# A decoder of two layers on one core: the order of work at four stage fronts

## The reference, cut to what matters

```
layer 0: causal self attention, 16 heads of 16, rotary factor on q and k
         GEGLU with the context as weights
         mixture: 1 shared + 8 routed experts (width 512), top 2, silu(x w1) * (x w3) @ w2
layer 1: full self attention, 16 heads of 16
         cross attention to the context (softmax over the queries)
         mixture: 8 experts (width 1024), top 2 with a masked softmax ("phi" routing)
```

## Time and profile before

| | |
|---|---|
| median of 3 runs | 1590.3 us (1586.99 to 1592.11) |
| profiled execution | 1590.26 us, of which the span of the trace 1588.5 us |
| mean granted TensorE clock | 0.948 |
| TensorE busy | 1417.9 us (89%) |
| VectorE busy | 1176.2 us (74%) |
| ScalarE busy | 908.1 us (57%) |
| GpSimd (POOL) busy | 635.8 us (40%) |
| DMA | 194.60 MB, mean 123 GB/s |

### The profile page before, as it was taken

One profiled execution on the slowest core, in us unless ns is written; L12 is line 12 of the kernel. 1 busy time (PEld: TensorE's weight loads), 2 busy tenths in 40 slices (PEclk: granted clock), 3 DMA queues, 4 the chain that ended last, 5 costly groups with the idle time before them and its releaser, 6 DMA issues. The chain is left out here.

```text
span 1588.5 us, 30443 instructions
## 1 busy us (share of the span) xinstructions
PE 1417.9 (89%) x10014; PEld 1000.2 (63%) x10014; DVE 1176.2 (74%) x2501; ACT 908.1 (57%) x1722; POOL 635.8 (40%) x899
## 2 busy tenths in 40 slices
PE   7899998989899999679999999898757899999997
PEld 3455554559899999424444433333245899999997
DVE  4777662554778888378788849998868688888885
ACT  1455553223256666136675678998813577766673
POOL 6565530010225665475554452553314233332221
PEclk8799998998999999869999999999987999999999
DMA  6223210220359887443223331332034687887882
GB/s 172 50 57 62 62 42 16 65 93 34 104 149 255 247 243 210 117 100 61 53 49 55 61 74 42 74 74 64 17 133 136 199 245 240 234 242 230 235 236 68
DMA packets 104571, 194.60 MB, mean 123 GB/s; under 512 B 30465, under 2 KB 55937, under 8 KB 101473
## 3 DMA queue, kind: packets, MB, share of 16 engines
q1 hardware_dynamic: 71760, 154.23, 31.2%
q0 software_dynamic: 31872, 37.79, 13.5%
q10 hardware_dynamic: 784, 0.66, 0.1%
HBM read 135.89 MB, written 18.61 MB: 97 GB/s over the span
## 5 line engine op out<-in xcount | busy, mean ns | idle before, releaser
L878 ACT ACTIVATE l1a_sb_probs<-l1a_s_ps,l1a_sb_kmax 128x512 f32<-128x512 f32 x256 | 172.5, 709 | 18.6 <-DVE l1a_sb_kmax L801 17.7
L766 DVE TENSOR_REDUCE l1a_sb_mx<-l1a_s_ps 128x2 f32<-128x1024 f32 x128 | 153.4, 1218 | 36.5 <-PE l1a_s_ps L982 36.4
L801 DVE TENSOR_REDUCE l1a_sb_kmax<-l1a_s_ps 128x1 f32<-128x512 f32 x256 | 160.5, 677 | 20.4 <-PE l1a_s_ps L1021 19.7
L884 ACT ACTIVATE l1a_sb_probs<-l1a_s_ps 128x1024 f32<-128x1024 f32 x128 | 130.1, 1024 | 72.6 <-PE l1a_s_ps L1021 72.0
L1021 PEld LDWEIGHTS l1a_s_ps<-l1a_sb_qst,l1a_sb_kst 49*128 49x128 f32 (+1 forms) x512 | 48.7, 189 | 163.8 <-issue 87.9
L761 DVE CUSTOM_DVE_ANT_0 l0a_sb_seen<-l0a_s_ps,l0a_sb_above 128x128 f32<-128x128 f32 (+3 forms) x256 | 113.5, 487 | 51.5 <-PE l0a_s_ps L982 51.2
L630 POOL DMA_DIRECT2D l1a_sb_kst<-l1a_sb_hi x228 | 112.8, 498 | 86.7 <-PE l1a_s_ps L1021 80.6
L2137 PE MATMUL l1m_g_ps<-l1m_sb_rows_hi,l1m_sb_hi 128*128 128x256 f32 x512 | 146.8, 287 | 0.4 <-DVE l1m_sb_late L2027 0.4
L2137 PE MATMUL l1m_g_ps<-l1m_sb_rows_lo,l1m_sb_hi 128*128 128x256 f32 x512 | 145.3, 284 | 0.0
L2137 PE MATMUL l1m_g_ps<-l1m_sb_rows_hi,l1m_sb_lo 128*128 128x256 f32 x512 | 145.3, 284 | 0.0
L1021 PE MATMUL l1a_s_ps<-l1a_sb_qst,l1a_sb_kst 49*128 49x512 f32 (+1 forms) x512 | 125.3, 498 | 21.4 <-ACT l1a_sb_probs L878 19.2
(11 more groups left out here) (437 smaller groups left out, 4011.5 us busy)
## 6 DMA issues: line engine op xcount, KB each, us to landing
l1m_sb_raw<-in_l1m_w SPq DMA_DIRECT2D x92, 512.0 KB, 4.6
l0m_sb_raw<-in_l0m_w SPq DMA_DIRECT2D x72, 512.0 KB, 4.8
l1m_sb_raw<-in_l1m_w SPq DMA_DIRECT2D x23, 1024.0 KB, 6.2
l1a_sb_qst<-l1a_sb_hi SPq DMA_DIRECT2D x256, 32.0 KB, 2.1
l1a_sb_kst<-l1a_sb_hi POOLq DMA_DIRECT2D x228, 32.0 KB, 2.0
l0a_sb_qst<-l0a_sb_hi SPq DMA_DIRECT2D x128, 32.0 KB, 2.2
l1a_sb_qst<-l1a_sb_lo SPq DMA_DIRECT2D x128, 32.0 KB, 2.1
l0a_sb_kst<-l0a_sb_hi POOLq DMA_DIRECT2D x124, 32.0 KB, 2.1
```

Source lines behind the costliest of these rows:

```text
L766: dve.tensor_reduce(mx[:, g, qt, 2 * p:2 * p + 2], buffer("A", b, g, j)[:, :, :], AX.X, ALU.max).then_inc(a_max.sem, 1)
L801: dve.tensor_reduce(kmax[:, n % 4, e:e + 1], buffer("S", b, g, j)[:, e, :], AX.X, ALU.max, negate=True).then_inc(kmax_done.sem, 1)
L878: ins = act.activation(probs[:, n % 8, e, :], at[:, e, :], ACT.Exp, bias=kmax[:, n % 4, e:e + 1], accum_out=zsum[:, n % 4, e:e + 1])
L884: act.activation(probs[:, n % 8, :, c0:T], at[:, :, c0:T], ACT.Exp, scale=SCALE).then_inc(exp_done.sem, 1)
```

## The change

1. *Attention, both layers.* Some `A` steps of group 1 are issued around the first `M`: in layer 0 four behind it; in layer 1 two before it and three behind it. The other 12 (11) of the 16 are spread evenly over the 8 `S` steps of the first slot. The warming matmuls become a step of their own, `WARM`, behind these, and are 5 and not 8.
2. *Layer 1's mixture, routing.* `UNMASKED 0` and `EXP 0` come directly behind `RANK`. The last five instructions of `EXPERTS` are a step `BLOCKS`, which with `LOAD` comes behind the last `SPOT`. `UNMASKED 1` comes before the first splits of weights, and `SHARES` and `WEIGHTS` come behind `T 0`. In both mixtures two of the four `held` instructions go from POOL to ScalarE (`held_in_tile`).
3. *Layer 1's mixture, loads.* `spots[0]` lies in `x`, whose copy to the sum must then have been read. SP fetches quarters 0 and 1 of w1 and w3, waits until the first block's rows have come, and fetches quarters 2 and 3 and, directly behind, w2.
4. *Layer 1's mixture, splits.* Quarters 0 and 1 are split before `T 0`, quarter 2 before `G 0 0`, quarter 3 in chunk (0, 0), w2 in two halves in chunks (0, 1) and (0, 2). The next set's quarters follow in chunks (0, 1), (0, 3), (1, 0) and (1, 1), the set after that in (1, 2) and (1, 3), two each. `WEIGHED` and the lists of part 2 move to behind chunks (0, 3) and (0, 2). `C` is cut in `CHI` (ScalarE) and `C` (VectorE), `CV` likewise.

```diff
...
+def ahead_of_slots(kinds):
+    return ("behind",) * 4 if kinds[0] == "causal" else ("before",) * 2 + ("behind",) * 3
...
-            for n in (2 * j, 2 * j + 1):
+            ahead = len(ahead_of_slots(kinds))
+            for n in range(ahead + j * (16 - ahead) // 8, ahead + (j + 1) * (16 - ahead) // 8):
...
+    ahead = ahead_of_slots(kinds)
+    for j, place in enumerate(ahead):
+        if place == "before":
+            yield "A", 0, 1, j
+    for j, place in enumerate(ahead):
+        if place == "behind":
+            yield "A", 0, 1, j
+    yield "WARM", 0, 0, 0
...
-                if b == 0 and g == 0:
-                    keep_warm(pe, o_ps[:, :], const, 8)
+            def warm(*_):
+                keep_warm(pe, o_ps[:, :], const, 5)
...
-                 "M": max_rows, "Z": turn, "N": turn_back})
+                 "M": max_rows, "WARM": warm, "Z": turn, "N": turn_back})
...
+        yield "CHI", 0, 0
+            yield "CHI", 0, f
-        yield "CV", 0, 0
+        for f in range(nf):
+            yield "CVHI", 0, f
+            yield "CV", 0, f
...
-                   5: [("EXP", 0, 0), ("EXPERTS", 0, 0), ("LOAD", 0, 0)],
+                   5: [("EXP", 0, 0), ("EXPERTS", 0, 0), ("BLOCKS", 0, 0), ("LOAD", 0, 0)],
...
-        for step in ("TOP1", "TOP2", "RANK", "EXPERTS", "LOAD", "ROWS", "PLACES", "HELD"):
+        for step in ("TOP1", "TOP2", "RANK", "UNMASKED", "EXP", "EXPERTS", "ROWS", "PLACES", "HELD"):
-        yield "UNMASKED", 0, 0
-        yield "EXP", 0, 0
+        yield "BLOCKS", 0, 0
+        yield "LOAD", 0, 0
-        yield "C", 0, 0
-        yield "SHARES", 0, 0
-        yield "WEIGHTS", 0, 0
+        yield "CHI", 0, 0
+        yield "C", 0, 0
+        yield "CHI", 0, 1
+        yield "C", 0, 1
-        yield "C", 0, 1
-        between = {1: [("LIST", c, 2) for c in range(NSPOT)] + [("WEIGHED", 0, 0)], nf: [("CV", 0, 0)]}
+        yield "SHARES", 0, 0
+        yield "WEIGHTS", 0, 0
+        yield "CHI", 0, 2
+        yield "C", 0, 2
+        between = {2: [("LIST", c, 2) for c in range(NSPOT)], 3: [("WEIGHED", 0, 0)]}
...
-            return (1, f - 1) if f else (1,)
+            return (1, 1) if f == nf - 1 else (1,)
+        if nf > 2 and n == 1:
+            return ((1, 2), (1, 3), (2, 0, 1), (2, 2, 3))[f]
...
-        if nf > 2 and n == 1 and f == 0:
-            yield from prepared(1, nf - 1)
-        if nf > 2 and n == 0 and f < 2:
-            yield "C", 0, f + 2
+        if nf > 2 and n == 0 and f == 0:
+            yield "CHI", 0, 3
+            yield "C", 0, 3
+        if nf > 2 and n == 0 and 0 < f < 3:
+            for part in (2 * f - 2, 2 * f - 1):
+                yield "CVHI", 0, part
+                yield "CV", 0, part
...
+        if nf > 2 and n == 0 and f == 1:
+            yield from prepared(1, 0)
...
-                     for t in (raw2[:, 0, :, :].rearrange("p f d -> p (f d)"),
+                     for t in (x[:, 0:NTILE // 2, :].rearrange("p n d -> p (n d)"),
...
-        placed, tokens_held = sem("placed"), sem("tokens_held")
+        placed, tokens_held, in_tile_held = sem("placed"), sem("tokens_held"), sem("in_tile_held")
...
+                    if f == 2 and not shared:
+                        sp.wait_ge(rows_in[0], halves_to(0) * 16)
+                if not shared:
+                    load_w2(s, e)
...
-            def first_w2(*_):
-                if not shared:
-                    sp.wait_ge(weights_listed, 1)
-                    load_w2(0, expert(0))
-            def second_w2(*_):
-                if not shared:
+            def second_w2(_, f):
+                if not shared and f == NF - 1:
...
-                 "CV": second_w2, "WEIGHED": first_w2, "Y": begin_sum})
+                 "CV": second_w2, "Y": begin_sum})
...
-                in_tile = const["token"][:, 0:1].unsqueeze(2).to_broadcast([P, NTILE, NBLK])
-                    for n, part in enumerate((tile_first, in_tile)):
-                        pool.tensor_tensor(held[:, k, :, n, :], own[:, k, :, :], part, ALU.mult).then_inc(tokens_held, 1)
+                    pool.tensor_tensor(held[:, k, :, 0, :], own[:, k, :, :], tile_first, ALU.mult).then_inc(tokens_held, 1)
...
+            def held_in_tile(*_):
+                act.wait_ge(placed, 1)
+                for k in range(TOP):
+                    act.activation(held[:, k, :, 1, :], own[:, k, :, :], ACT.Copy, scale=const["token"][:, 0:1]
+                                   ).then_inc(in_tile_held, 1)
...
-            def first_w2(*_):
-                for f in range(NF):
-                    split_w2(0, f)
...
-            run({"END": end, "TURN": turned_rows, "EXP": exp, "T": rows_of, "C": split_w13, "CV": first_w2, "W": next_w13,
+            run({"END": end, "TURN": turned_rows, "HELD": held_in_tile, "EXP": exp, "T": rows_of, "CHI": split_w13, "CVHI": split_w2, "W": next_w13,
...
-                                 weights_listed=weights_listed, weighed=weighed, weights_known=weights_known, placed=placed))
+                                 weights_listed=weights_listed, weighed=weighed, weights_known=weights_known, placed=placed,
+                                 summed=summed))
...
-            def first_w2(*_):
-                for f in range(NF):
-                    rest_w2(0, f)
...
-            run({"END": end, "LN1": ln, "LN2": normal, "T": rows_of, "C": rest_w13, "CV": first_w2,
+            run({"END": end, "LN1": ln, "LN2": normal, "T": rows_of, "C": rest_w13, "CV": rest_w2,
...
-                    pe.wait_ge(tokens_held, 2 * (c * SPOTS // NTILE + 1))
+                    pe.wait_ge(tokens_held, c * SPOTS // NTILE + 1)
+                    pe.wait_ge(in_tile_held, c * SPOTS // NTILE + 1)
...
+    def blocks(*_):
+        end = full("end")
...
+        if c == 0 and phi:
+            dve.wait_ge(sems["summed"], 16)
...
-    return {"TOP1": top1, "TOP2": top2, "UNMASKED": unmasked, "EXPERTS": experts, "SHARES": shares, "ROWS": rows,
+    return {"TOP1": top1, "TOP2": top2, "UNMASKED": unmasked, "EXPERTS": experts, "BLOCKS": blocks, "SHARES": shares, "ROWS": rows,
```

## The result

| | kernel before | kernel after |
|---|---|---|
| median of 6 runs each, first comparison | 1590.72 us (1586.69 to 1597.77) | 1581.44 us (1576.60 to 1583.66) |
| second comparison | 1594.00 us | 1578.64 us (1578.02 to 1582.96) |
| third comparison | 1595.02 us | 1578.14 us (1575.54 to 1583.88) |

The ratio of the first comparison is 0.9915, 95% interval [0.9888, 0.9943]; of the second 0.9912 [0.9879, 0.9944]; of the third 0.9905 [0.9873, 0.9937]. So the kernel is faster by 0.6 to 1.3%: 9.3, 15.4 and 16.9 us by the three pairs of medians, 13.8 on average, where 16.6 were forecast. 1581.44 us lies in the range of 1567 to 1583, but not in the 1568 to 1578 that the prediction gave for the forecast alone; it is 7.7 us above 1573.7.

The account below looks back on a forecast made before the run. TensorE's work was taken to bound the end behind layer 1's first `Y`, VectorE to cause the stop before it. 10.5 + 0.5 + 4.5 + 1.1 = 16.6 us off 1590.3 gave 1573.7 us; range 1567 to 1583.

Parts of the forecast that it names:

- the attention gives nothing: Rival, layer 1's first group: TensorE at clock 0.50 may set the pace, some 1 us gained, warmers cost it; 1578.7, chance 0.14.
- Layer 1's mixture: Routing to first `Y`: earlier `T 0`, shorter stop and no low clock behind it give 10.5 us, bounds 7 and 12.
- The loads that collide with the gather: Rival, layer 1's mixture: gather 3 us and w2 another 2 later, giving 5.5 not 10.5 us; 1578.7, chance 0.16.
- Layer 0's mixture: Gate maybe 0.9 us later, spots freed by POOL's shorter work: 0.5 us gained, bounds 1 lost, 1.1 gained.
- Layer 0's attention: Behind the first group's norm, 6 pairs in place of 8: 1.1 us gained, bounds 1 lost, 2 gained.
- Layer 1's attention: First group: maxima fill VectorE's idle wait before the first `S`; 4.5 us gained, bounds 1 lost, 5.9 gained.
- The 2.3 us before the norm: Layer 1's first group: 4 maxima in place of 6 up to `LN2`, so the norm starts 2.3 us earlier.
- The 2.4 us behind the norm: Layer 1's first group: 7 maxima in place of 10, 3.5 us of VectorE, about two thirds taken as gain.
- The low clock lasts: slower: Rival, both attention fronts and `T 0` to `Y 0`: fewer warmers leave clock 0.50; 10 us slower, 1601, chance 0.06.

Follow-up runs that it names:

- the two kernels with the early row: Kernel after with `M` of the second group at step 1: 1585.68 us; the same plus quarter 1 of w13 split behind `T 0`: 1586.95 us.

## Why the prediction was right, and which term was off

The kernel is faster by 13.8 us in the mean of three comparisons, where 16.6 were forecast. The mixture bore the sum out; the attentions did not, and a measurement of 1578 to 1581 us by itself would fit the rival "the attention gives nothing" (1578.7) at least as well as the forecast.

- **Layer 1's mixture: forecast 10.5 us, measured 11.7** (432.2 and 432.3 in two profiles of the old mixture, 420.5 on average of seven of the new, 420.0 to 421.5). The steps, in the first profile: spots 1.42 and 1.13 us, `LISTS` 2.67, first `Y` at 1229.7 us for 1230.4, a stop of 1.45 us for 1.0, 1.6 us more from the higher clock. `T 0` came 4.4 us earlier and not 2.7: the half gather that it waits for took 2.9 us from its issue, where before it took 4.6. But the first `G` came only 3.7 us earlier, held by the split of the rows, which I had not listed as a wait. That the first `Y` was met to 0.7 us is in part luck: `T 0` gave 1.7 us more than forecast, and the work from `T 0` to the stop took 1.1 us less, at a clock of 1.00 from `T 0` to the first `Y`, where before had 0.88; against that stand 1.6 us of waits that were not forecast and 0.45 us more of stop. The rest of the gain is the time behind the first `Y`, 347.1 us in place of 349.2; of those 2.1 us, 1.6 are the clock.
- **The loads that collide with the gather** did not. 250 of the 256 packets of the two quarters had gone when the gather's first began, and `T 0`'s wait fell from 2.3 to 0.9 us. Something of the rival is there: the gather's first packet came 2.9 us behind its issue, where before it was 1.8.
- **Layer 0's mixture: forecast 0.5 us, measured 0.** It and the GEGLU ahead of it took 382.2 us before and after.
- **Layer 0's attention: forecast 1.1 us.** The stage ends at 272.6 to 274.4 us, 273.5 on average of nine profiles of the new order, against 274.8 and 273.3 with the old: about 0.6 us, less than the spread.
- **Layer 1's attention: forecast 4.5 us, and this is the term that was mis-sized.** Where the long wait for the row is absent, the third split is at 46.3 to 46.6 us with the new order (four profiles) and 47.8 with the old (two): 1.3 us. With the long wait it is 48.8 to 49.5 (four) and 50.3 (one): 1.1 us. The 2.3 us before the norm were 1.46: `M` to the first `S` took 5.3 us for 4.9, and the maximum that was to follow at once waited 0.90 us for TensorE. Of the 1.46, 0.83 went into a longer norm. The 2.4 us behind the norm were 0.7 (1.3 less the 0.63 left at the norm's end). I had taken two thirds of VectorE's saved maxima, but behind the norm TensorE sets the pace. The row of 698 to 708 us shows it:

```profile
698.00:708.00 10.00, 6.51 (x26) 3.30 (x30) 7.73 (x9) 5.10 (x8) 7.35 (x6) 0.50 0.48 123
```

  TensorE's 6.51 us of work here are one unbroken piece from 701.49 us on. The 3.49 us ahead of it are the wait of 3.62 us for the norm: the transposes stand in its queue ahead of the next pairs of scores, so it can't work ahead. Behind the norm VectorE, busy 7.73 us, waits for TensorE. My rival said that TensorE at the low clock may set the pace and gave 1 us; it was the better description behind the norm, and not ahead of it. All of this is read from rows: no kernel changed the clock or the place of the transposes, so what the low clock has to do with it is not shown.
- **The low clock lasts: slower.** The first `G` took 3.14 us and the window from 1218 to 1237 us had a clock of 1.00, where the earlier trace rows have 0.93 five us earlier. Not so in this mixture.

Together the traces give 11.7 + 0 + 0.6 + 1.3 = 13.6 us; the three pairs of medians average 13.8. That they agree so well is chance too, as the pairs differ from one another by 7.6 us.

What stays open is the 2 to 3 us wait. All four transfers of the row have their data by 726.9 us in after, and TensorE starts at 728.96, 2.1 us later; in before 0.6 us lie between. A transfer of instructions of 16 KB lies beside the row's transfers in all five executions that have the long wait, and starts 5 to 6 us ahead of the first of them in the other six. This is the DMA view of 723 to 727 us in after; in before, the same view of that stretch has no such line, and the view of 717 to 722 us has it:

```profile
q8 instruction: 1, 0.02, 1.8%
```

```profile
q8 instruction: 1, 0.02, 1.2%
```

Kernels that differ from after only in later code fall on both sides, and the kernel after fell on the same side three times in three. So the side isn't settled by the code up to there, nor by the new order of the attention; what settles it is open. Whether the load makes the wait was not shown either. In the two kernels with the early row such a load lies beside its transfers as well; there the row goes out earlier, and TensorE doesn't wait for it.

## What to carry to other kernels

A stop ahead of the first instruction of a long steady phase is worth its length, plus the low clock behind it: read which queue ends last there and take work out of it, down to the point at which the order no longer matters. A gain in a front that feeds another pipeline is to be priced by what the other engine allows, at the clock that it has there: here, with TensorE 83% and VectorE 93% busy, 1.3 us of 4.5 arrived. And one profiled execution is no measure of a stage's change: the same kernel's stage took 499.3, 499.6 and 506.6 us, so a stage is compared over several executions, and within it by distances between instructions that the change touches.

## What the hardware did that I had not expected

- VectorE's bf16 spots (0.27 us each) took 5.39 to 5.40 us for 16 beside four instructions of 0.80 us on POOL, 4.27 beside two, 3.21 beside none. Each POOL instruction costs VectorE 0.5 to 0.6 us: in before, the four spots beside them last 0.77 to 0.84 us and start 0.76 us apart, the others 0.20 apart, so that one spot gets through for each POOL instruction and 0.56 us are lost. Two of them were worth 1.12 us, for which I had forecast 1.1. The Trainium skill (SBUF — State Buffer, Who interferes with whom) says that the two block each other for the whole instruction. The trace agrees as far as a spot ends 0.08 us behind the POOL instruction beside it; the price of 0.80 us each that I took from it is not what the runs show.
- The norm's four instructions took 2.45 us where POOL's second `w_lo` pass lay beside the first of them (1.48 us, the others 0.40), and 3.28 us where both passes of about 1.3 us lay beside them: then two took 1.34 us each.
- The cross attention shows low-clock periods of 3 to 11 us (in after 999 to 1002 and 1053 to 1064 us, in its second execution none there) which come and go between executions of one kernel. Laid beside the second execution, the two cost 1.5 and 2.6 us.
